# Twelve-layer fp32 network on one core: row sums of 16-head attention taken from TensorE, mask and maximum in one VectorE instruction, turned copies shared in the last attention

## The reference, cut to what matters

```python
# layer 5 (L1_xattn)
score = jnp.einsum('nqhd,nkhd->nhqk', q, k)
score = jnp.where(mask == 0, jnp.float32(-1e+20), score)
attn = jax.nn.softmax(score / jnp.sqrt(jnp.float32(D)), axis=-1)
out = jnp.einsum('nhqk,nkhd->nqhd', attn, v).reshape(n, lq, H * D)
return out @ Wo.T + bo
# layer 4 (L1_attn): scores = relu(q k) * R_hat, causal, softmax, times v
# layer 8 (L2_xattn): logits = q k / 16 + mask * -1e9, softmax, times v
# layer 11 (L3_xattn): q and k scaled, masked, 512 keys (256 of the context, 256 of x), softmax, times v, Wo, layernorm
```

## Time and profile before

| what | value |
|---|---|
| median of three runs | 3718.55 us (3714.8 to 3731.33) |
| the profiled execution | 3732.82 us, its span 3731.0 us |
| mean granted TensorE clock | 0.905 of full speed |
| TensorE matmul busy | 2976.7 us (80%) |
| VectorE busy | 2299.4 us (62%) |
| ScalarE busy | 1749.1 us (47%) |
| GpSimd busy | 747.6 us (20%) |

### The profile page before, as it was taken

How to read it: one execution, slowest core, us unless ns; L and a number is a source line. 1 busy time by engine, 2 the same in 40 slices (tenths; PEclk the granted TensorE clock), 3 DMA queues, 4 the chain that set the end, 5 groups by cost and what they waited for, 6 DMA issues and landing times. The chain is left out here.

```text
span 3731.0 us, 54776 instructions
## 1 busy us (share of the span) xinstructions
PE 2976.7 (80%) x18517; PEld 2127.6 (57%) x18517; DVE 2299.4 (62%) x5176; ACT 1749.1 (47%) x4238; POOL 747.6 (20%) x865
## 2 busy tenths in 40 slices
PE   6999999998776895676877654595799848888797
PEld 5777777776565583454554324244596435555485
DVE  6777667775566335776777786897311675555423
ACT  6666666665421222776677262403332325555121
POOL 2111111110101421354444000000110003333422
PEclk8999999999898997898899777798799979999799
DMA  3111111111002583000000000000696010000476
GB/s 119 43 46 38 35 35 49 43 35 40 18 1 77 178 294 130 1 1 15 16 7 1 26 0 0 3 0 12 235 343 221 23 49 13 24 24 12 159 257 212
DMA packets 109524, 264.81 MB, mean 71 GB/s; under 512 B 16928, under 2 KB 71456, under 8 KB 104384
## 3 DMA queue, kind: packets, MB, share of 16 engines
q1 hardware_dynamic: 92896, 229.01, 18.4%
q0 software_dynamic: 8688, 23.78, 1.7%
q10 hardware_dynamic: 7664, 8.51, 0.7%
HBM read 213.72 MB, written 47.54 MB: 70 GB/s over the span
## 5 line engine op out<-in xcount | busy, mean ns | idle before, releaser
L1296 POOL TENSOR_TENSOR L3x_p<-L3x_p,L3x_rsum 128x512 f32<-128x512 f32 x128 | 133.0, 1040 | 448.1 <-DVE L3x_rsum L1377 448.1
L3025 POOL TENSOR_TENSOR L0a_sum_sq<-L0a_sum_sq,L0a_sq 128x512 f32<-128x512 f32 x56 | 73.1, 1305 | 698.7 <-ACT L0a_sq L2944 698.7
L2847 ACT ACTIVATE L0a_ex<-bank,L0a_nb 128x128 f32<-128x128 f32 x512 | 145.2, 367 | 126.1 <-PE bank L2776 125.6
L3113 DVE TENSOR_TENSOR L0a_ru<-bank,L0a_um 128x512 f32<-128x512 f32 x128 | 88.2, 689 | 182.1 <-PE bank L2768 167.2
L3104 DVE SCALAR_TENSOR_TENSOR L0a_xf<-L0a_xc,L0a_conv,L0a_xf 128x256 f32<-128x256 f32 x432 | 178.7, 482 | 9.1 <-ACT L0a_xf L2909 7.7
L1358 DVE SCALAR_TENSOR_TENSOR L3x_s<-bank,L3x_bias 128x512 f32<-128x512 f32 x128 | 86.4, 681 | 134.3 <-PE bank L1136 134.3
L1986 PE MATMUL bank<-L2a_half,L2a_diag 128*128 128x512 f32 x328 | 144.1, 601 | 28.4 <-ACT L2a_diag L1969 28.4
L1296 POOL TENSOR_TENSOR L1x_p<-L1x_p,L1x_rsum 128x512 f32<-128x512 f32 x128 | 132.2, 1040 | 138.6 <-DVE L1x_rsum L1377 138.6
L1300 POOL TENSOR_TENSOR L1a_p<-L1a_p,L1a_rsum 128x128 f32<-128x128 f32 (+1 forms) x256 | 123.0, 506 | 137.7 <-DVE L1a_rsum L1377 135.6
L2690 PE MATMUL bank<-x_feat,L0a_wx 128*128 128x256 f32 x576 | 138.1, 391 | 4.1 <-ACT L0a_xc L2896 4.1
L2776 PE MATMUL bank<-L0a_ru,L0a_vm 128*128 128x512 f32 x256 | 137.6, 621 | 0.0
(11 more groups left out here) (727 smaller groups left out, 8215.8 us busy)
## 6 DMA issues: line engine op xcount, KB each, us to landing
L2f_wt<-in_L2f_w SPq DMA_DIRECT2D x23, 2180.0 KB, 10.2
L0f_wt<-in_L0f_w SPq DMA_DIRECT2D x39, 898.0 KB, 6.7
L3f_wt<-in_L3f_w SPq DMA_DIRECT2D x39, 768.0 KB, 5.0
L0a_wx<-in_L0a_wx SPq DMA_DIRECT2D x72, 256.0 KB, 3.1
L0a_wz<-in_L0a_wz SPq DMA_DIRECT2D x32, 512.0 KB, 4.1
context_keys_values<-L2f_zeros ACTq DMA_DIRECT2D x32, 256.0 KB, 4.9
L0f_xs<-rows_by_expert SPq DMA_DIRECT2D x39, 128.5 KB, 3.4
L3f_xs<-rows_by_expert SPq DMA_DIRECT2D x39, 128.5 KB, 2.8
```

The source lines that it names most:

```text
L1296: last = nc.gpsimd.tensor_tensor(both, both, rsum[r % 2][:, i, :].unsqueeze(2).to_broadcast([P, S, NK]), ALU.mult)
L2847: last = a(ex[g % 3][:, j, b * P:(b + 1) * P], bank[:, at:at + P], ACT.Exp, bias=nb[r % 2][:, b, h:h + 1])
L3113: rv.empty(vec.tensor_tensor(ru[g % 2][:], bank[:].rearrange("p (j t) -> p j t", j=2), um[:].unsqueeze(1).to_broadcast([P, 2, T]), ALU.mult))
```

## The change

It does five things.

1. In the 16-head layers the probabilities stay unnormalised. `weigh` has, beside each matmul with the values, one with a new tile `summing` (ones in the columns of one twin, zeros in the other's), so that half of the accumulation bank holds the row sums, in the layout of the weighed values. After each second step (`half`) ScalarE copies the bank to `raw`, VectorE inverts its sum half (`inverse`, 128x256) and GpSimd multiplies the two halves into `cT`. The 256 accumulator outputs of a layer's exponentials, the 128 small reciprocals and the 128 multiplications of probabilities are gone. TensorE waits for the copy `raw` before each second `weigh`, and turns an item when its exponential is done. `output` comes one step later.
2. Outside layer 4, `scale_mask` and `maximum` become one `tensor_tensor_reduce` per tile of queries (in layer 8 too). The order below prints it as an ISA row and a second ISA row that writes `nmax` alone. ScalarE's exponential takes scale -1.
3. The fourth turned copy of a step is taken by VectorE behind the first `scale_mask` of a step, not the third. In layer 11, which had no such copy, VectorE now takes the second of each two.
4. In the 16-head layers the part q comes before the part k (`UNITS`).
5. The loop of one turn and the copies `xb` and `cb` are gone; matmuls read `x_feat` and `ctx_feat` themselves.

The diff, without the change of indentation:

```diff
-        UNITS = [[("k", 0)], [("q", 0)], [("v", 0)], [("v", 1)]]
+        UNITS = [[("q", 0)], [("k", 0)], [("v", 0)], [("v", 1)]]
...
-    by_dve = lambda key: twins == 2 and key[0] == "p" and key[1] % G == G - 1
+    by_dve = lambda key: key[0] == "p" and key[1] % G == G - 1
...
+                    for e in range(twins):
+                        for other in range(twins):
+                            nc.gpsimd.memset(summing[:, e, other * DV:(other + 1) * DV], 1.0 if other == e else 0.0)
...
-        with nc.Fori(0, B // ROWS) as turn:
...
                 def transposes(j):
                     bank = claim(("p", j))
+                    if twins == 2:
+                        pe.wait_ge(sig("exp"), S * (j + 1))
+                    else:
                         pe.wait_ge(sig("divided"), j + 1)
...
                 def weigh(u):
                     r, first = divmod(u * G, n)
-                    if first == 0 and r:
+                    if twins == 2 and u % 2 == 0 and u:
+                        pe.wait_ge(sig("raw"), u // 2)
+                    if twins == 1 and first == 0 and r:
                         pe.wait_ge(sig("cT"), n_cT * r)
...
                     for kt in range(KT):
+                        for of in range(twins):
                             for d in range(G):
...
-                                    out = acc[0][rows_out, tile * T + at:(tile + 1) * T]
+                                    out = acc[0][rows_out, of * T + at:(of + 1) * T]
+                                    weights = summing[:, e, :] if of else weights
...
-                            if step == 0 and r:
+                        if step == twins - 1 and r:
                                 output(r - 1)
                             weigh(u - LA - 1)
...
+                def half(i):
+                    act.wait_ge(sig("weighted"), 2 * (i + 1))
+                    if i >= 2:
+                        act.wait_ge(sig("cT"), i - 1)
+                    nc.scalar.activation(raw[i % 2][:], acc[0][:], ACT.Copy).then_inc(sig("raw"), 1)
...
-                        act.wait_ge(sig("max"), g + 1)
+                    act.wait_ge(sig("max") if causal else s_ring.emptied, g + 1)
                         for e, (t, at, nk) in enumerate(items[i][1]):
                             nc.scalar.activation(p_sb[g % NP][:, at:at + nk], s_sb[g % NSB][:, at:at + nk], ACT.Exp,
-                                                 bias=nmax[r % 2][:, i, e:e + 1],
-                                                 accum_out=rsum[r % 2][:, i, e:e + 1]).then_inc(sig("exp"), 1)
+                                             bias=nmax[r % 2][:, i, e:e + 1], scale=1.0 if causal else -1.0,
+                                             accum_out=rsum[r % 2][:, i, e:e + 1] if twins == 1 else None).then_inc(sig("exp"), 1)
...
                     for u in range(steps + LA):
                         r, step = divmod(u, PER_ROW)
+                    if twins == 2 and u > LA + 2 and (u - LA) % 2 == 1:
+                        half((u - LA - 3) // 2)
...
+                if twins == 2:
+                    for i in range(2 * ROWS):
+                        pool.wait_ge(sig("reciprocal"), i + 1)
+                        if i >= 2:
+                            pool.wait_ge(sig("projected"), i // 2)
+                        nc.gpsimd.tensor_tensor(cT[:, i % 2, :], raw[i % 2][:, 0:T], raw[i % 2][:, T:2 * T], ALU.mult).then_inc(sig("cT"), 1)
...
-                            ins = vec.scalar_tensor_tensor(out=s[:], in0=bank[:, 0:W], scalar=scale,
-                                                           in1=bias[r % 2][:].rearrange("p t s -> p (t s)"), op0=ALU.mult, op1=ALU.add)
+                        for e, (t, at, nk) in enumerate(items[i][1]):
+                            ins = vec.tensor_tensor_reduce(out=s[:, at:at + nk], in0=bank[:, at:at + nk], in1=bias[r % 2][:, e, :],
+                                                           scale=-scale, scalar=3e38, op0=ALU.add, op1=ALU.min,
+                                                           accum_out=nmax[r % 2][:, i, e:e + 1])
...
+                def inverse(i):
+                    dve.wait_ge(sig("raw"), i + 1)
+                    below = raw[i % 2][:, T:2 * T]
+                    vec.reciprocal(below, below).then_inc(sig("reciprocal"), 1)
...
                         if twins == 2:
                             if d == 0 and g < total:
                                 scale_mask(g)
+                        if d == 0 and u > LA:
+                            take_turned((u - LA) * G - 1)
                             if d < G - 1 and g < total:
                                 scale_mask(g + 1)
-                            if d == 1 and u > LA:
-                                take_turned((u - LA) * G - 1)
...
                         if i == (LA + 2) * G and 0 < r < ROWS and kind == "latent":
                             spread(r - 1)
+                    if twins == 2 and d == G - 2 and u > LA + 2 and (u - LA) % 2 == 1:
+                        inverse((u - LA - 3) // 2)
+                    if twins == 2 and i == G - 1 and r >= 2:
+                        output(r - 2)
+                    if twins == 1 and i == (LA + 3) * G and 0 < r < ROWS:
                             output(r - 1)
-                        if RLAG <= g < total + RLAG:
+                    if twins == 1 and RLAG <= g < total + RLAG:
                             reciprocal(g - RLAG)
                         if twins == 1 and g + 1 < total and d < G - 1:
                             scale_mask(g + 1)
-                        if g < total:
+                    if twins == 1 and d == 0 and u > LA:
+                        take_turned((u - LA) * G - 1)
+                    if causal and g < total:
                             maximum(g)
```

More of the change, by code:

```diff
@@ new lines, in weigh @@
+                                last = nc.tensor.matmul(out, weights, come_from, start=(e == 0 and kt == 0 and of == 0),
+                                                        stop=(e == twins - 1 and kt == KT - 1 and of == twins - 1))
+                    last.then_inc(sig("weighted"), 1)
+                for what, i in in_order:
+                    project(0, what, i)
+                for u in range(-1, steps + LA + 1):
+                    own = range((u - LA) * G, (u - LA + 1) * G) if LA <= u < steps + LA else []
+                    for j in own[:G // 2]:
+                        transposes(j)
+                    if u > LA:
+                        r, step = divmod(u - LA - 1, PER_ROW)
+                        if step == twins - 1 and r:
+                            output(r - 1)
+                        weigh(u - LA - 1)
+                    if 0 <= u < steps:
+                        for r, what, i in units_at(u):
+                            project(r, what, i)
+                    if u + 1 < steps:
+                        r, step = divmod(u + 1, PER_ROW)
+                        if step == 0:
+                            key = ("q", r, MQ // 2 - 1)
+                            pe.wait_ge(t_emptied(key), n_emptied[key])
+                            pe.wait_ge(sig("k_taken"), K_UNITS * (r + 1))
+                            if kind == "latent":
+                                pe.wait_ge(sig(f"kv{r % 2}"), 32 * (r // 2 + 1))
+                        scores(u + 1)
+                    for j in own[G // 2:]:
+                        transposes(j)
@@ L1453, in _ @@
-                    if kind == "latent":
-                        spread(ROWS - 1)
-                    output(ROWS - 1)
-            sig.clear()
-        sig.close()
+                        vec.tensor_tensor(y[:], proj, rowwise(bo), ALU.add).then_inc(sig("out_read"), 1)
+                        dve.wait_ge(sig("out_read"), r + 1)
+                    vec.tensor_tensor(xr, xr, y[:], ALU.add).then_inc(sig("added"), 1)
+                hide(0)
+                for what, i in in_order:
+                    if what == "k":
+                        project(0, i)
@@ L1461, in layer1_attn @@
+                if twins == 2:
+                    inverse(2 * ROWS - 1)
+                if kind == "latent":
+                    spread(ROWS - 1)
+                output(ROWS - 1)
+        sig.clear()
+    sig.close()
 def layer1_attn(c):
```

630 lines of the change are left out of this document (283 added, 347 removed).

## The result

The changed kernel takes 3756.92 us (median of 7 runs, 3745.0 to 3763.94), the kernel before 3730.21 us (7 runs, 3714.8 to 3738.67) beside it: 1.007 times the time, 95% interval 1.005 to 1.0091. It is 27 us slower where 48 were forecast. The profiled executions are 3732.82 and 3756.92 us (spans 3731.0 and 3755.1), a difference of 24.1 us in the spans.

| part | before, us | after, us | difference | forecast |
|---|---|---|---|---|
| layer 4 | 289.2 | 277.6 | -11.6 | -5 |
| layer 5 | 316.9 | 298.6 | -18.3 | -7 |
| layer 8 | 53.8 | 53.6 | -0.2 | -3 |
| layer 11 | 410.6 | 467.8 | +57.2 | +63 |
| all others | 2660.5 | 2657.5 | -3.0 | 0 |

A forecast was written before the change was run, and what follows sets the result against it. Layers 4, 5 and 11 were taken as bound by a ring through several engines, none full. Layer 11 +63, layer 5 -7, layer 4 -5, layer 8 -3 gave +48 on 3718.55: 3766 us, forecast 3735 to 3790 (0.57), range 3706 to 3798.

The forecast's parts named there:

- The masking's price T: Layer 11: a fused masking with its accumulator read takes 0.76 us; weighing starts at 1.97 + 2T, costing 50 us.
- my lower bound of 0.61: Layer 11: lowest price of a fused masking, the old masking's own spacing; the upper end was 1.22 us.
- spacings far from 0.76: Layer 11: fused maskings spaced far from 0.76 us would prove the forecast wrong.
- What stands ahead of the copy: Layer 11, once in each of 7 rows: statistics (1.14 us), then normalisation and additions (3.29), delay VectorE's copy; +24 us.
- The output and the copies `xb`: Layer 11: ScalarE reaches `cT` before TensorE asks, -17 us; the copies of `xb` at the start go, -2.
- Layers 4 and 5: Earlier turned copy shortens steps, doubled weighing and every second step's wait for `raw` lengthen them; -5 and -7 us.
- the 27 and 31 us that I had named as a sign: Rows of layers 4 and 5 below these lengths would prove the wait for `raw` wrong.
- GpSimd's multiplications: 16-head layers: the 128 multiplications a layer cost nothing before, so taking them away gives nothing.
- Layer 8: Masking and maximum become one: up to 5.6 us, but half the items wait for TensorE anyway; -3 us.
- That sharing the copy helps: Rival, layer 11: the copy is off the path and relieving ScalarE gains, kernel some 3680 us; needs T below 0.29; chance 0.12.
- The rival of the clock: Layer 11: short waits bring TensorE to 1.2 GHz, +37 us, 3803; with a dear fused instruction, 3790 to 3810, chance 0.14.
- That the 16-head layers gain more: Rival: no wait for `raw` appears and T is at its lower end; 3719 to 3737 us, chance 0.17.

## Why the prediction was right, and where its terms were off

The sign, its place and its mechanism held: layer 11 loses because weighing now waits for a copy that stands behind two maskings, and the 16-head layers gain less than that. The experiments, taken one upon the other, split the 57.2 us of layer 11: -20.1 without the copy on VectorE, -4.3 with it at the head of the step, +42.2 with statistics and additions ahead of it, +39.4 with the second masking too.

- *The masking's price T.* I took 0.76, nearest to a masking with a small instruction behind it. By the same reckoning it is 0.62 and 0.60: the second masking starts 0.69 us behind the first and the copy 0.60 behind the second, and 0.07 of the 0.69 is the small reciprocal, which the sum has on its own. That is my lower bound of 0.61, a read that costs nothing; I had called spacings far from 0.76 a sign against the forecast, and this term did fail by that sign. From the end of the copy to weighing pass 0.14 us, where I had 0.06. Weighing starts at 3.28, not 3.49, so a step is 0.73 longer and not 0.94: 53 x 0.73 = 39 instead of 50. (The experiments' 39.4 is another sum: 32 for one masking, and clock.)
- *What stands ahead of the copy.* 24 + 10 for the clock were forecast; 42.2 was measured, 27.5 of it idle time and 14.7 clock. The idle times are as the rows gave them: TensorE waits 2.28 us in the step of the statistics and 4.41 in that of the additions, where a plain step has 1.13, so 1.15 and 3.28 more. But the clock took more than 1.40 us a row: in the step above the matmuls of weighing and of the keys lost 0.89 and 1.79, and in four of six full rows the step of the statistics lost 1.4 to 1.7 as well (7.37 us where it lost nothing).
- *The output and the copies `xb`.* -17 - 2 against -24.4, which is the 20.1 and the 4.3 that the copy taken off ScalarE gives in the output step. So the terms were off by -11, +8 and -5, and their sum is +57 for the +63 that I put down. That they cancel so far is luck.
- *Layers 4 and 5.* Steps of 5.6/6.6 and 6.7/7.7 were forecast, 5.48/6.41 and 6.54/7.48 came; weighing twice as many matmuls costs 0.86, not 1.00, and the output 1.82, not 2.0 to 2.2. So the rows are 27.2 and 31.5 for 28.2 and 32.8, and 18 of the 24 us by which the forecast was too high (48 against 24.1 in the spans) lie here. The weighing that waits for `raw` was right to 0.02 us (4.57 and 4.55). The rows came just above the 27 and 31 us that I had named as a sign against the wait for `raw`; the trace shows that wait, 0.87 us in layer 5 and 0.90 in layer 4.
- *The reason that I gave for their gain* was incomplete. I took the change as a whole; the runs show that the place of VectorE's copy and the fused masking gain 16 us in layer 4 and 36 in layer 5, the removal of `xb`, `cb` and the loop some 10 in each, where I had counted next to nothing for the copies themselves, and that the row sums on TensorE take 15 and 27 back.
- *GpSimd's multiplications* cost nothing before, and taking them off gained nothing: right, and more so, since with them the kernel is faster.
- *Layer 8.* -3 forecast, -0.2 measured: a row of two items takes 5.82 us in either kernel, with TensorE idle 1.69 us until VectorE has made its next copy of the context, which no masking holds up.
- *The rivals.* That sharing the copy helps is false where it was put (T was 0.61, far above 0.29), and true where it stands first. There the Trainium skill's advice in *TensorEngine Tiling (Array Packing)*, section PSUM Bottleneck, to empty PSUM with both engines, fits the run with the copy first: 386.2 us against 390.5 with ScalarE alone. The place of the copy is worth 81.6 us here. The rival of the clock did not come: the plain steps wait 1.13 us each and still weigh in 1.09, at full clock. That the 16-head layers gain more came in part, -29.9 us for -12, but with the wait for `raw`, whose absence was that rival's condition. And the row sums were more than idle work saved elsewhere: they cost 15 and 27 us.

## What to carry to other kernels

Which engine has time to spare decides less than what stands ahead of the new instruction in that engine's list, above all the long work that comes once a row. When a change has several parts, cost each against a kernel that has all the others: here a part that lost 42 us in two layers was carried by two that gained more. And when a part of a wait goes, look at the clock of the matmuls behind it: in layer 4, 0.51 us less of waiting for `cT` came with 1.32 us less of output. The other way round, a copy that came earlier made a wait of 0.80 us into one of 1.69, and the output behind it 1.3 us longer.

## What the runs showed of the hardware that was not expected

- The fused masking, minimum included, runs as fast as the masking alone: 0.69 us against 0.69 at 128x512, and 0.42 against 0.42 at 128x256. The read of its accumulator (0.08 us) starts with the next instruction and adds nothing to the spacing (3197.09 in the plain step above):

```profile
L1362 DVE DVE_READ_ACCUMULATOR2_ANT L3x_nmax<- x128: 81/84/85, 3047.9 to 3461.2; 128x1 f32 x128
```

- The releaser that the profile names can be the wrong one of two copies that end 0.11 us apart. The gap between the end of a copy and the start of weighing, 0.14 us in both kernels, spoke for VectorE's, and the run with the copy between the maskings showed it.
- With the wait for `cT` in layer 4 at 1.18 us and not 1.69, the 8 matmuls behind it took 1.97 us and not 3.29. The wait alone doesn't tell the clock: weighing behind the wait of 2.28 us in layer 11 takes 1.09 to 1.98 us, from row to row of one execution.
